# A four-layer language model tower on one core: gates through DRAM, weights rounded in the first stage, fewer and wider steps in the quantized attention

## The reference

```python
# embedding: a table row, a position row, one of two type rows
segment_ids = jnp.cumsum(sep_ids, axis=1) - sep_ids
return token_emb + pos_emb[None, :, :] + one_hot(segment_ids, 2) @ token_type_emb_table

# quantized attention, ahead and behind the heads
x_int, s_x = _act_quant(x)             # one scale: max |x| / 127 over all of x
wq_int, s_wq = _weight_quant(w_qkv)    # one scale per output row
acc_s = s_x * s_wq
qkv_int = jnp.einsum('bnc,oc->bno', x_int, wq_int) + round(b_qkv / acc_s)
s_qkv = max(|qkv_int * acc_s|) / 127   # over everything
...
out_int = jnp.einsum('bnc,oc->bno', ctx8, wp_int) + round(b_proj / out_s)
return out_int * out_s

# codes block: S = 8 subspaces of R = 16, M = 64 codes each, the best K = 4, hidden H = 32
z = einsum('nd,sdr->nsr', xf, P); scores = einsum('nsr,smr->nsm', z, C)
topv, topi = top_k(scores, K); w = softmax(topv)
h = gelu(einsum('nsr,nskrh->nskh', z, W1[s, topi]) + b1[s, topi])
yl = einsum('nskh,nskhr->nskr', h, W2[s, topi]) + b2[s, topi]
comb = einsum('nskr,nsk->nsr', yl, w)
out = gelu(comb @ G1 + g1b) @ G2 + g2b
```

## Time and profile before

| | us |
|---|---|
| median of 3 runs (3580.55 to 3584.8) | 3582.79 |
| profiled execution | 3578.07 |
| its span | 3576.3 |
| TensorE busy | 2556.9 (71%) |
| VectorE busy | 2419.3 (68%) |
| ScalarE busy | 1604.6 (45%) |
| GpSimd busy | 831.2 (23%) |
| mean granted TensorE clock | .83 of full |

### The profile page before, as it was taken

The page is one execution under the profiler, slowest core; times in us unless marked ns, Lnnn a source line. Parts: engine busy times, 40 slices in busy tenths (PEclk is TensorE's granted clock), DMA queues, the critical chain, the costliest instruction groups (busy, mean ns, idle before and its releaser), DMA issues. The chain is left out here.

```text
span 3576.3 us, 39626 instructions
## 1 busy us (share of the span) xinstructions
PE 2556.9 (71%) x13085; PEld 1566.8 (44%) x13132; DVE 2419.3 (68%) x5733; ACT 1604.6 (45%) x2888; POOL 831.2 (23%) x438
## 2 busy tenths in 40 slices
PE   3968995788888876699831113788989777785466
PEld 3955663333434333499621111322222366664345
DVE  4454336399999997211378996687787699998621
ACT  1111112566666652111217772677777545554211
POOL 1000000467676762367200001000000011111021
PEclk9768997899999997799955555899999888887678
DMA  1121001202020200511100001000000100000221
GB/s 37 19 80 45 1 1 31 91 4 95 0 95 0 95 0 1 165 40 40 46 10 0 1 1 44 13 1 1 1 1 1 30 1 1 1 1 1 67 110 50
DMA packets 59444, 109.35 MB, mean 31 GB/s; under 512 B 32045, under 2 KB 47755, under 8 KB 53995
## 3 DMA queue, kind: packets, MB, share of 16 engines
q1 hardware_dynamic: 53484, 95.04, 8.2%
q0 software_dynamic: 5760, 11.82, 1.1%
HBM read 92.76 MB, written 18.03 MB: 31 GB/s over the span
## 5 line engine op out<-in xcount | busy, mean ns | idle before, releaser
L1938 POOL TENSOR_TENSOR mam_st<-mam_du,mam_b_rows 128x1536 f32<-128x1536 f32 x128 | 439.5, 3441 | 172.7 <-PE mam_ysum L2007 172.2
L2168 DVE TENSOR_TENSOR_SCAN mam_st<-mam_da,mam_st 128x512 f32<-128x512 f32 x384 | 441.0, 1204 | 35.9 <-ACT mam_da L2108 18.2
L1716 DVE TENSOR_TENSOR cod_hp<-cod_hp,cod_gate 128x512 f32<-128x512 f32 x512 | 324.2, 682 | 123.0 <-ACT cod_hp L1583 121.0
L2007 PE MATMUL mam_ysum<-mam_st,held_ident 128*128 128x512 f32 x768 | 391.5, 650 | 2.2 <-DVE mam_st L2174 2.2
L1583 ACT ACTIVATE cod_hp<-cod_up,cod_b 128x512 f32<-128x512 f32 x512 | 319.2, 693 | 130.7 <-PE cod_up L1454 130.1
L2108 ACT ACTIVATE mam_da<-mam_delta,mamw_decay 128x508 f32<-128x508 f32 x384 | 254.1, 683 | 184.2 <-DVE mam_st L2168 149.5
L2282 POOL TENSOR_TENSOR att_probs<-att_se,att_neg 128x1536 f32<-128x1536 f32 x16 | 55.0, 3440 | 999.7 <-DVE att_neg L2487 999.7
L2174 DVE TENSOR_TENSOR mam_st<-mam_st,mam_c_ps 128x1536 f32<-128x1536 f32 x128 | 224.4, 1753 | 16.9 <-PE mam_c_ps L2002 13.4
L2007 PEld LDWEIGHTS mam_ysum<-mam_st,held_ident 128*128 128x128 f32 x768 | 159.9, 208 | 168.6 <-issue 161.5
L489 DVE SCALAR_TENSOR_TENSOR held_h<-x_dn,held_gate,held_h 128x192 f32<-128x192 f32 x256 | 89.1, 410 | 183.8 <-PE x_dn L456 182.1
L1459 PE MATMUL cod_gate<-cod_wt,cod_sel_g 128*128 128x512 bf16 x465 | 181.6, 391 | 39.4 <-DVE cod_hp L1716 38.8
(11 more groups left out here) (523 smaller groups left out, 5484.2 us busy)
## 6 DMA issues: line engine op xcount, KB each, us to landing
mam_b_rows<-b_scratch SPq DMA_DIRECT2D x32, 1024.0 KB, 6.8
sw_w<-in_L_w SPq DMA_DIRECT2D x2, 4608.0 KB, 33.2
gr_w<-in_L_w SPq DMA_DIRECT2D x1, 5376.0 KB, 43.3
gr_w<-in_L_w SPq DMA_DIRECT2D x1, 4608.0 KB
slot_scratch<-in_slot_fresh SPq DMA_DIRECT2D x1, 3860.0 KB
gr_rows<-slot_scratch SPq DMA_DIRECT2D x40, 96.5 KB, 1.9
x1w_w<-in_L_w SPq DMA_DIRECT2D x1, 3072.0 KB
gr_w<-home_scratch SPq DMA_DIRECT2D x16, 192.0 KB, 4.4
```

The source lines that it names most:

```text
L1716: nc.vector.tensor_tensor(at, at, gate[u % BANKS][:], ALU.mult).then_inc(gated, 1)
L1938: nc.gpsimd.tensor_tensor(st[it % N_ST][:], du[r % 2][:], along(b_rows[:, p % RING, n % PIECE, :], 1, [P, MC, MT]), ALU.mult)\
L2007: last = nc.tensor.matmul(ysum[:, c, :], m.ident[:], st[it % N_ST][:, c, :], start=False, stop=(it % DS == DS - 1))
L2168: nc.vector.tensor_tensor_scan(fs, fa, fs, 0.0, ALU.mult, ALU.add).then_inc(scanned, 1)
```

## The change

Five places are changed:

- Codes: of the four units of a step only j = 0 and 1 (QP = 2) keep a gate product. The weights of the other subspaces are turned in f32 (`turn_gates`, two turns of 512 columns per group, steps 23 and 24), copied to `turned_gates`, and written to DRAM by SP, four transfers (`send_gates`, behind the reads of step 28, and ahead of the loop for group 0). For each step SP reads them back with one transfer that repeats each row for 32 SBUF rows (`bring_gates`, 512 KB), into a ring of five (`wide_gates`). VectorE multiplies units 2 and 3 by that tile. There are four `up` and two `gate` banks. Units 2 and 3 of a step work on the same code column as its k. `wt` and the bf16 parts `wp` are half as wide, the turns of 1024 columns are four instead of eight (steps 25 to 28), and the b2 products are 12 small bf16 ones and two f32 ones.
- Embedding: position row plus first type (16 operations on VectorE, into `base`) and second type (16 copies on ScalarE, into `second`) are computed without the gathered rows and added (3072 columns); the gathered rows of each group are then added in one operation, when that group's gathers are in. The rounding, turning and scale row of the quantized attention's weights are done in this stage, ahead of that on VectorE and ScalarE, and written to DRAM; norm n4 reads them back by `ahead`.
- Norms with a router: the second part is turned once, and ScalarE writes it out twice (three copies per group instead of one).
- Projections: one stage instead of two. Rounding of `xn` by groups of four tiles, unrolled loops, no copies on GpSimd, three banks. VectorE adds the bias per tile, and takes the maximum per column over four tiles (a reduction over a strided view of 2304 elements); scale row and the last maximum come once behind.
- Output: rounding by groups, unrolled, no copies on GpSimd, three operations of 768 columns per group instead of three of 192 per tile.

```diff
+            sp.dma_start(q_w[:], a["Q_w"]).then_inc(q_in, 16)
...
+            act.wait_ge(seg_split, 1)
+            for b in range(NB):
+                last = nc.scalar.activation(second[:, b, :], types[:, 1, :], ACT.Copy, scale=seg_is[:, 1, b:b + 1])
+            last.then_inc(second_ready, 1)
...
+            v.wait_ge(q_in, 16)
+            c.step(nc.vector.tensor_reduce(q_max[:], q_w[:], AX.X, ALU.max, apply_absolute_value=True))
+            scale_steps(nc, c, q_scale[:], q_inv[:], q_max[:])
+            v.sem_inc(q_scaled, 1)
+            full = [DC, WC, D]
+            c.step(nc.vector.tensor_tensor(q_w[:], q_w[:], along(q_inv[:], 2, full), ALU.mult))
+            v.wait_ge(consts_in, 80)
+            c.step(nc.vector.tensor_copy(m.bf_ident[:], m.ident[:]))
+            quant_steps(nc, c, q_int[:], q_w[:], None, q_work[:])
+            v.sem_inc(q_ready, 1)
...
-            v.wait_ge(rows_in, 16 * NB)
-            v.wait_ge(consts_in, 80)
-            c.step(nc.vector.tensor_tensor(m.h[:], m.h[:], along(pos[:], 1, [P, NB, D]), ALU.add))
-            c.step(nc.vector.tensor_copy(m.bf_ident[:], m.ident[:]))
-            for t in range(2):
-                for b in range(NB):
-                    last = nc.vector.scalar_tensor_tensor(m.h[:, b, :], types[:, t, :], seg_is[:, t, b:b + 1],
-                                                          m.h[:, b, :], ALU.mult, ALU.add)
-                c.step(last)
+            v.sem_inc(seg_split, 1)
+            for b in range(NB):
+                last = nc.vector.scalar_tensor_tensor(base[:, b, :], types[:, 0, :], seg_is[:, 0, b:b + 1], pos[:],
+                                                      ALU.mult, ALU.add)
+            c.step(last)
+            v.wait_ge(second_ready, 1)
+            c.step(nc.vector.tensor_tensor(base[:], base[:], second[:], ALU.add))
+            for g in range(NG):
+                at = slice(g * GS, (g + 1) * GS)
+                v.wait_ge(rows_in[g], 16 * GS)
+                last = nc.vector.tensor_tensor(m.h[:, at], m.h[:, at], base[:, at], ALU.add)
+...
                         nc.tensor.transpose(bank[:, 0, at], x[:, 0:P], m.ident[:])
-                        for row in (0, D - P):
-                            last = nc.tensor.matmul(bank[row:row + D - P, 1, at], x[:, P:D], m.ident[:], start=True,
-                                                    stop=True)
+                        last = nc.tensor.transpose(bank[0:D - P, 1, at], x[:, P:D], m.ident[:])
...
-                    nc.scalar.activation(wide[:, :, g * GT:(g + 1) * GT], turned[g % RING][:], ACT.Copy)\
-                        .then_inc(cols_ready, 1)
+                    cols = slice(g * GT, (g + 1) * GT)
+                    nc.scalar.activation(wide[:, 0, cols], turned[g % RING][:, 0], ACT.Copy)
+                    for row in (0, D - P):
+                        last = nc.scalar.activation(wide[row:row + D - P, 1, cols], turned[g % RING][0:D - P, 1],
+                                                    ACT.Copy)
+                    last.then_inc(cols_ready, 1)
...
-BANKS = 3
+BANKS = 4
+GBANKS = 2
 HOLD = 3
+QP = 2
+QD = QS - QP
+NSP = 2 * QP
+GRING = 5
+SEND_AT = 28
...
-    return (k % HT + 2 * j) % HT
...
+    return (k % HT + 2 * j) % HT if j < QP else k % HT
...
+            def send_gates(g):
+                if g == 0:
+                    sp.wait_ge(first_kept, FIRST_GF + 2)
+                else:
+                    sp.wait_ge(misc_kept, prep_turn(g) + GF_AT + 2)
+                for half in range(2):
+                    for j in range(QD):
+                        sp.dma_start(m.gate_scratch[g % 2, half].rearrange("c e j t -> (c e) j t")[:, j],
+                                     turned_gates[j * SM:(j + 1) * SM, half, :]).then_inc(gates_out, 16)
+
+            def bring_gates(g, k):
+                step = g * STEPS + k
+                if step >= GRING:
+                    sp.wait_ge(gated, QS * (step - GRING + 1))
+                sp.dma_start(wide_gates[:, step % GRING].rearrange("p j t -> p (j t)"),
+                             along(m.gate_scratch[g % 2, k // HT, k % HT].rearrange("e j t -> e (j t)"), 1,
+                                   [ET, SH, QD * GT])).then_inc(gates_in[step % GRING], 16)
+
+            sp.wait_ge(w1_split, 1)
+            send_gates(0)
+            for g in range(NG):
+                sp.wait_ge(gates_out, 16 * 2 * QD * (g + 1))
+                for k in range(STEPS):
+                    bring_gates(g, k)
+                    if k == SEND_AT and g + 1 < NG:
+                        send_gates(g + 1)
...
+            def turn_gates(g, half, bank, ready):
+                pe.wait_ge(weighted, GS * (g + 1))
+                for t in range(GS):
+                    at = t * SS + half * QS + QP
+                    last = nc.tensor.transpose(bank[:, t * P:(t + 1) * P],
+                                               ex[:, at:at + QD, :].rearrange("p n e -> p (n e)"), m.ident[:])
+                last.then_inc(ready, 1)
+
...
-                if u >= BANKS:
-                    pe.wait_ge(gated, u - BANKS + 1)
+                if j >= QP:
+                    return
+                if u >= QS:
+                    pe.wait_ge(gated, u - QS + 1)
                 half, code = f // NBLK, f % NBLK
-                nc.tensor.matmul(gate[u % BANKS][:], sel_g[:, code, :], wt[g % 2][:, 2 * sub + half, :],
+                nc.tensor.matmul(gate[j][:], sel_g[:, code, :], wt[g % 2][:, 2 * (QP * (k // HT) + j) + half, :],
                                  start=True, stop=True).then_inc(gate_ready, 1)
...
-                        for j in range(QS):
-                            sub = QS * half + j
-                            nc.tensor.matmul(comb[32 * j:32 * j + 32, :], b2_part[q // 2][:, 2 * sub + q % 2, :],
-                                             wt[g % 2][:, 2 * sub + q % 2, :], start=(q == 0), stop=False)
+                        for j in range(QP):
+                            n = 2 * (QP * half + j) + q % 2
+                            nc.tensor.matmul(comb[32 * j:32 * j + 32, :], b2_part[q // 2][:, n, :],
+                                             wt[g % 2][:, n, :], start=(q == 0), stop=False)
+                    for j in range(QD):
+                        rows, at = slice(j * SM, (j + 1) * SM), 32 * (QP + j)
+                        nc.tensor.matmul(comb[at:at + 32, :], b2d[rows, half, :], turned_gates[rows, half, :],
+                                         start=True, stop=False)
...
-                        if 24 <= k:
-                            misc_turn(turn + WT_AT + k - 24)
-                            turn_w(g + 1, k - 24, misc, misc_ready)
+                        if 23 <= k < 25:
+                            misc_turn(turn + GF_AT + k - 23)
+                            turn_gates(g + 1, k - 23, misc, misc_ready)
+                        if 25 <= k < 29:
+                            misc_turn(turn + WT_AT + k - 25)
...
-                v.wait_ge(gate_ready, u + 1)
                 at = hp[step % HOLD][:, j, :]
-                nc.vector.tensor_tensor(at, at, gate[u % BANKS][:], ALU.mult).then_inc(gated, 1)
+                if j < QP:
+                    v.wait_ge(gate_ready, QP * step + j + 1)
+                    by = gate[j][:]
+                else:
+                    v.wait_ge(gates_in[step % GRING], 16 * (step // GRING + 1))
+                    by = wide_gates[:, step % GRING, j - QP, :]
+                nc.vector.tensor_tensor(at, at, by, ALU.mult).then_inc(gated, 1)
...
+            for g in range(NG):
+                at = slice(g * GS, (g + 1) * GS)
+                quant_steps(nc, c, z.x_int[:, at], m.xn[:, at], x_inv[:, 0:1], x_work[:, at])
+                v.sem_inc(x_ready, 1)
+            v.wait_ge(z.w_in, 48)
...
+            for t in range(NB):
+                v.wait_ge(acc_ready, t + 1)
+                c.step(nc.vector.tensor_tensor(z.qkv[:, t].rearrange("p (a n) -> p a n", a=2),
+                                               acc[t % NACC][:, :, 0:N],
+                                               z.bias_row[:].rearrange("p (a n) -> p a n", a=2), ALU.add))
+                v.sem_inc(summed, 1)
+                if t % GS == GS - 1:
+                    g = t // GS
+                    c.step(nc.vector.tensor_reduce(parts[:, g], z.qkv[:, g * GS:t + 1].rearrange("p t n -> p n t"), AX.X,
+                                                   ALU.max, apply_absolute_value=True))
+            c.step(nc.vector.tensor_reduce(most[:], parts[:].rearrange("p g n -> p n g"), AX.X, ALU.max))
+            c.step(nc.vector.tensor_tensor(most[:], most[:], z.acc_row[:], ALU.mult))
+            nc.vector.tensor_reduce(all_max[:], most[:], AX.X, ALU.max).then_inc(maxed, 1)
             v.wait_ge(shared, 1)
...
-            quant_steps(nc, c, c8[:], z.ctx[:], ns[:, 0:1], work[:])
-            v.sem_inc(c8_ready, 1)
+            for g in range(NG):
+                at = slice(g * GS, (g + 1) * GS)
```

(11 more changed lines are left out.)

375 lines of the change are left out of this document (173 added, 202 removed).

## The result

The changed kernel takes 3691.7 us (median of 4 runs, 3689.63 to 3693.21) against 3581.67 for the kernel before (median of 4 runs; the table above has three of them): a ratio of 1.0306, 95% interval 1.0291 to 1.0321. It is slower by 110 us, where 100 us less were forecast, and the time lies far outside the range of 3445 to 3525. One term of the sum failed by far more than all others together, and it is the one that was costed at nothing.

What follows compares the result with a forecast made beforehand. No engine bounds the whole span; the loop's plain step is a ring of waits. Savings 62.5 + 3.0 + 7.6 + 3.0 + 13.8 + 10.3 = 100.2 us take the median from 3582.79 to 3482, range 3445 to 3525.

Steps and rivals of the forecast that it cites:

- The new transfers: Code loop: each step's 512 KB gate read at 430 GB/s takes 1.2 us, hidden under the step, costed at nothing.
- plain step: Code loop, steps doing only up, gelu, gate and down: 3.19 us falls to 2.48, VectorE the bound, .71 saved each.
- Rival (B): Code loop: gate transfers are the bound at 127 GB/s, 4.1 us per step, total 3553; decides below 211 GB/s; chance .08.
- the norm: First norm: second identity product per tile goes, the first becomes a transpose; 3 us saved (0 to 4.5).
- the output: Quantized attention's output: 48 operations in 22.65 us become four groups of three 768-wide ones, 11.2; 10.3 saved (8 to 11.5).
- Rival (C): Code loop: TensorE's clock held at 1.2 GHz, a step 4.6 us instead of 2.48, total 3614; chance .03.
- last quarter: Code loop's last group, 107.40 us: 26 plain steps save 18.5, six other steps 2.6, together 21.1.
- a preparing quarter: Code loop, first three quarters, also preparing the next group: stretches save 5.0, 1.0, 3.7 and 4.1; 13.8 each, 41.4 together.
- (A): Code loop: VectorE packs, heavy steps' work slides into light ones; loop 410, 110 saved, total 3435; chance .22.
- (D): Code loop: the ring closes elsewhere, a step stays near 2.9, loop saves 25 to 45, total about 3510; chance .07.
- Embedding: Embedding stage: weights rounded early, base rows added apart from the gathers; end at 31.2, 7.6 saved (2.8 to 13.5).
- Projections: Quantized attention's start and projections: weights' chain gone, one addition per tile, strided maxima 3.9 each; 13.8 saved (6.4 to 20.8).

Runs made afterwards that it cites:

- the kernel with four transfers: The changed kernel with each step's read of gates issued as four transfers of 32 SBUF rows instead of one of 128: 3483.93 us, ratio .9729.

## Why the prediction was wrong

**The step that failed is "The new transfers", costed at nothing.** Its rate, 430 GB/s, was taken from a broadcast that looks alike in bytes and in repeated rows. But that one has 128 rows outermost and works on 16 engines; the new one has four. Its real price is 5.09 us per step, 652 us for 128 steps, where the loop without it gives a cover of 459.1, 2.40 in a plain step and 3.6 on average. The loop took 201.7 more than with the reads in four (660.8 against 459.1). The other end of the bound, 127 GB/s, stood in the same group and was put aside.

**Rival (B) was the case**, at a chance of .08. Its mechanism and its point of decision (211 GB/s) held: 103 lies below it, and at the 210 GB/s of the four reads, about what a plain step consumes, VectorE waits for no transfer. Its price was too small, 3553 against 3691.7, since the rate was taken from the row of 127 and not derived from the shape of the transfer. Whoever had counted 4 × 27 GB/s, one DMA engine's part in the earlier trace rows for each outermost row, would have had 108 GB/s and 4.9 us.

**The range** stopped at 3525 although the bounds named for that term, 430 and 127 GB/s, reach 3553. It should have taken them in. Two of the small terms left their own bounds as well: the norm with 9.5 (0 to 4.5) and the output with 7.3 (8 to 11.5). The chances for slower were wrong too: (B) was priced only to 3553, and so counted as faster.

**Rival (C)**, the clock: it did fall, to .82 over the loop, but behind the transfers. With them hidden it was .95 and the time that of the forecast.

**The rest of the codes stage came out in its sum**, 63.8 of 65.5 us, as the kernel with four transfers shows. The plain step is right in size and mechanism; the split of a preparing quarter is not:

- plain step 2.48 forecast, 2.40 measured, with VectorE never idle as forecast; last quarter 107.4 − 21.1 = 86.3 forecast, 87.4 measured;
- a preparing quarter 13.8 less forecast; the three gave 13.5, 11.5 and 14.6. By stretches of the second, as in the earlier trace rows, the split is another one: 2.7, 1.4, 1.9 and 5.5 for the 5.0, 1.0, 3.7 and 4.1 of the forecast. Errors of both signs cancelled. The first and the last stretch in the kernel with four transfers:

```profile
2379.00:2412.20 33.20, 30.75 (x158) 10.64 (x157) 21.63 (x36) 22.84 (x40) 0.00 (x0) 1.00 0.50 140
...
2481.00:2504.40 23.40, 21.66 (x145) 6.87 (x144) 20.69 (x36) 23.40 (x40) 0.00 (x0) 1.00 0.75 199
```

TensorE's work in the first fell to 30.75 as forecast (30.9), but 2.4 us of idle stand beside it, where the kernel before had 1.5 and the forecast none; in the last ScalarE, the engine named for it, has 23.40 of 23.40, the work as forecast (23.2) and the 1.6 of idle gone that the forecast kept. What the remaining idle of the first stretch waits for was not tested;
- (A), packing to VectorE's own work, didn't happen: the loop takes 459.1 us and not 410. Nor did (D): the plain step is 2.40 and not 2.9.

That this kernel lands 2 us from the forecast is again partly luck: its codes stage and the four stages ahead give 100.0 us of the 100.2 forecast, with +6.5 for the norm and −.8, −1.2, −3.0 and −1.7 for the others.

**Embedding**: 6.8 against 7.6. ScalarE's sixteen copies took 5.62 us (.35 each, not .30). The last gather was stretched, 3.59 instead of .95 us, while VectorE's addition of 3072 columns ran:

```profile
24.86 3.36 DVE L207 TENSOR_TENSOR emb_base<-emb_base,emb_second 128x3072 f32<-128x3072 f32 x1 [5.55 <-ACT emb_second L179]
...
28.26 3.56 DVE L211 TENSOR_TENSOR held_h<-held_h,emb_base 128x768 f32<-128x768 f32 x4
```

```profile
25.45 3.59 POOL L141 DMA_INDIRECT held_h<-in_table,emb_ids  x1 [0.30 <-issue]
```

The Trainium skill ("SBUF — State Buffer", section "SBUF: two separate sides") says that GpSimd waits while VectorE holds the port pair that both use, and that a VectorE operation with two SBUF inputs takes it against a GpSimd operation that reads SBUF. The rows agree: the addition has two inputs in SBUF, the gather reads its row numbers there, and it ended at 29.04, .82 us behind the addition. It was just early enough to do no harm: the four additions at the end run without a gap.

**Norm**: 9.5 against 3, the small term that was mis-sized most. It was taken from the products of the second part alone, but the turning of the first part got shorter beside them (.40 us from its start to the next product before, .21 after); the clock, which stood at .50 in the whole stage before, gave about 2.3; and the copies on ScalarE, which were to give part back, lay beside TensorE's work.

**Projections and output**: 12.6 against 13.8 and 7.3 against 10.3. In both the rounding by groups takes 7.8 us (four times .62, .56 and .56 with gaps) and not the 6.0 of the forecast; in the output it was left out of the sum altogether, where it adds 2.4. The 22.65 us of the output's operations also ran to the next stage's first operation, .8 us beyond their own end at 2200.15. The maxima took 4.18 each for 3.9.

## What to carry to other kernels

Before a transfer is costed at nothing, look at its shape, not at its bytes: the size of the outermost dimension says how many of the 16 DMA engines carry it, and a broadcast that puts 4 outside and the 32 repeats inside runs on 4. In the profile it shows as a DMA share that stands still at a round fraction (.25, .13) while an engine waits for the transfer. Cutting such a transfer helped when each part had 32 rows outermost; cut in two halves of two it was twice as slow.

A change whose parts lie in different stages can be read stage by stage between barriers, and a single wrong term does not speak against the others: with one transfer cut in four the same change gives −96 us in place of +110.

## What the runs showed of the hardware

- One DMA engine moved 24 to 27 GB/s in pieces of 2 to 8 KB, whether 2, 4 or 16 worked (52, 103 and 430 GB/s).
- With 16 engines and only two rows of 4 KB for each per transfer the rate per busy engine was 17 GB/s (210 GB/s at a share of .77). Why it is lower was not looked into.
- Two transfers issued one behind the other on SP's queue, each with two rows outermost, used the same two engines: 10.17 us for 512 KB. On the same queue a write with 64 rows outermost ran beside reads issued before it (share .85 for .7 us, .25 before and after).
- A transfer left one small packet for each engine that worked on it: 4, 2 and 16.
- Transposes of 128 and 64 columns in f32 followed each other at .21 us at the lower clock. Behind 3.7 us of them alone the granted clock was .98 for 2.7 us; in the kernel before, with two products with the identity beside each transpose, it stayed at .50 for the 21 us.
- A gather on GpSimd took 3.59 us instead of .95 while VectorE added two SBUF tiles of 3072 columns.
- A reduction over four elements in strides of 576 cost 4184 ns, over four neighbours 2553 ns.
